# Last stage of a float32 model kernel: matmuls on quarter and eighth tiles without zero halves, one sine operation, and one addition moved from POOL to PE

## The reference

```python
DIM = 128; DEPTH = 6; HEADS = 16; DIM_HEAD = 64; WINDOW = 32; QK_SCALE = 8.0
for i in range(DEPTH):
    x = attn_layer(shift_tokens(x), Wqkv[i], q_scale[i], k_scale[i], Wo[i]) + x
    x = ffn_layer(shift_tokens(x), ln_g[i], ln_b[i], W1[i], b1[i], W2[i], b2[i]) + x
# attn_layer, for q (and k with 1 / scale):
q = l2norm(q) * q_scale
q = q * cos * scale + rotate_half(q) * sin * scale
# local_attention: each window of 32 queries sees its own and the previous window's keys (64)
sim = einsum('bhwie,bhwje->bhwij', bq, bk2) * QK_SCALE      # masked
out = einsum('bhwij,bhwje->bhwie', softmax(sim), bv2)
```

## Time and profile before

| | us |
|---|---|
| median of 3 runs | 4824.44 |
| lowest, highest | 4803.81, 4836.79 |
| profiled execution, span from first to last instruction | 4799.2 |
| PE busy | 4554.0 (95%) |
| DVE busy | 3761.7 (78%) |
| POOL busy | 3692.6 (77%) |
| ACT busy | 3501.1 (73%) |

### The profile page before, as it was taken

How to read it: one execution, slowest core, us unless ns; L and a number is a source line. 1 busy time by engine, 2 the same in 40 slices (tenths; PEclk the granted TensorE clock), 3 DMA queues, 4 the chain that set the end, 5 groups by cost and what they waited for, 6 DMA issues and landing times.

```text
span 4799.2 us, 114895 instructions
## 1 busy us (share of the span) xinstructions
PE 4554.0 (95%) x44512; PEld 3128.6 (65%) x44512; DVE 3761.7 (78%) x5226; ACT 3501.1 (73%) x6738; POOL 3692.6 (77%) x2336
## 2 busy tenths in 40 slices
PE   7998999987887799999999999999999999999997
PEld 5666768874443466666666666666666666666665
DVE  6776556658999688888888888888888888888885
ACT  3454756557775688888888888888888888888885
POOL 2222334438998999999999999999999999999993
PEclk9898999998999999999999999999999999999998
DMA  2000000004332222232222322232322322322222
GB/s 79 1 2 1 2 1 1 1 1 168 150 142 106 55 63 63 56 85 70 54 67 65 75 68 55 68 75 61 68 64 67 76 53 66 80 64 63 62 56 52
DMA packets 164292, 289.06 MB, mean 60 GB/s; under 512 B 44063, under 2 KB 61351, under 8 KB 159655
## 3 DMA queue, kind: packets, MB, share of 16 engines
q1 hardware_dynamic: 162310, 281.46, 22.3%
q10 hardware_dynamic: 1440, 0.24, 0.0%
HBM read 90.22 MB, written 2.62 MB: 19 GB/s over the span
## 4 chain that ended last, share of the span: by engine, by line
PE 59%; ACT 3%; issue 2%; DVE 1%; POOL 1%; ACTq 0%; DVEq 0%; POOLq 0%
PE ps L2559 18%; PE ps L2614 8%; PE ps L2588 8%; PE ps L2572 7%; PE ps L2627 7%; PE ps L2601 3%; PE ps L2669 3%; PE ps L2660 3%; PE ps L2653 3%; ACT L3f_pT L2820 2%; PE ps L2634 1%; PE ps L2640 1%; ACT L3f_kT L2803 1%; POOL L3f_t L3155 0%; POOL L3f_raw L3172 0%
## 5 line engine op out<-in xcount | busy, mean ns | idle before, releaser
L3155 POOL TENSOR_TENSOR L3f_t<-L3f_raw,L3f_rot 128x512 f32<-128x512 f32 x768 | 1007.7, 1334 | 268.3 <-DVE L3f_raw L2971 268.3
L2559 PE MATMUL ps<-L3f_wqkv,all_z 128*128 128x512 f32 x2304 | 1133.7, 601 | 12.8 <-DVE L3f_raw L2971 11.7
L3172 POOL TENSOR_TENSOR L3f_raw<-L3f_raw,L3f_t 128x1024 f32<-128x1024 f32 x384 | 961.4, 2504 | 3.8
L3164 POOL TENSOR_TENSOR L3f_raw<-L3f_raw,L3f_rot 128x1024 f32<-128x1024 f32 x384 | 953.8, 2484 | 3.8
L2971 DVE TENSOR_TENSOR L3f_raw<-ps,L3f_ri 128x512 f32<-128x512 f32 x768 | 495.6, 682 | 231.9 <-ACT L3f_ri L2778 230.2
L2954 DVE TENSOR_REDUCE L3f_ss<-L3f_sqr 128x8 f32<-128x512 f32 x768 | 507.8, 681 | 163.2 <-ACT L3f_sqr L2768 160.8
L2572 PEld LDWEIGHTS ps<-all_ident,L3f_raw 128*128 128x128 f32 x3072 | 358.7, 141 | 320.7 <-issue 282.8
L2559 PEld LDWEIGHTS ps<-L3f_wqkv,all_z 128*128 128x128 f32 x2304 | 385.2, 191 | 221.0 <-issue 151.5
L2572 PE MATMUL ps<-all_ident,L3f_raw 128*128 128x128 f32 x3072 | 472.3, 276 | 49.1 <-ACT L3f_kT L2803 27.1
L2820 ACT ACTIVATE L3f_pT<-ps 64x512 f32<-64x512 f32 x768 | 453.2, 590 | 83.9 <-PE ps L2601 75.9
L2768 ACT ACTIVATE L3f_sqr<-ps 128x512 f32<-128x512 f32 x768 | 449.9, 599 | 76.5 <-PE ps L2559 71.7
(11 more groups left out here) (333 smaller groups left out, 8702.0 us busy)
## 6 DMA issues: line engine op xcount, KB each, us to landing
L3f_vw<-L3f_v SPq DMA_DIRECT2D x1344, 128.0 KB, 2.4
L3a_Bs<-L3a_rows SPq DMA_DIRECT2D x16, 2048.0 KB, 7.1
L3a_Cs<-L3a_rows SPq DMA_DIRECT2D x16, 2048.0 KB, 11.6
L3f_vw<-L3f_v SPq DMA_DIRECT2D x192, 64.0 KB, 2.1
L3f_wqkv<-in_L_ffn_Wqkv SPq DMA_DIRECT2D x24, 256.0 KB, 2.9
L3f_wqkv<-in_L_ffn_Wqkv SPq DMA_DIRECT2D x6, 512.0 KB, 3.6
L3f_wo<-in_L_ffn_Wo SPq DMA_DIRECT2D x48, 64.0 KB, 2.3
out<-all_x SPq DMA_DIRECT2D x8, 256.0 KB, 3.6
```

The lines of the kernel that those rows point to most:

```text
L2559: p.matmul(PS[:, j % 3, :], Z[:, u % NSEQ, t * P:t * P + P], w, start=True, stop=True).then_inc(proj.sem)
L3155: op = g.tensor_tensor(t[:, :, to], r[:, :, fr], w[:, 1, to].unsqueeze(1).broadcast_to((P, H, WIN)), ALU.mult)
L3164: g.tensor_tensor(r, r, w[:, 0, :].unsqueeze(1).broadcast_to((P, H, HD)), ALU.mult).then_inc(cosined.sem)
L3172: g.tensor_tensor(r, r, t, ALU.add).then_inc(rotated.sem)
```

## The change

- `qz` becomes `qT`, the transposed queries with no zeros, and `pT` likewise. `scores` now issues, for each pair of heads and window, one matmul per head: 64 rows by 32 columns of weights, 64 moving columns, output in 32 partitions, one PSUM bank per head. That is 64 matmuls instead of 32, over 2 x 4 = 8 different parts of the array. `values` issues 64 matmuls instead of 32: 64 rows by 64 columns of weights, 32 moving columns, over 2 x 2 = 4 parts.
- ACT's copy of queries is one operation of 128 partitions instead of two of 64, and `spread` one of 128 x 1024 instead of four of 64 x 512.
- The two operations of `sine` become one, which reads the two 32-wide blocks of each head in reverse order.
- For k1, POOL's `add` is gone. PE transposes the cosine part (in `raw`) and then the sine part (in a third buffer of `t2`) into the same place in PSUM, adding. `sine` of k1 now waits for PE's last transpose of k1 of the unit before.
- Mask, scores and probabilities have another order of heads, and the two memsets of zeros are gone.

```diff
-        t2 = self.sb("t2", [P, 2, INNER])
+        t2 = self.sb("t2", [P, 3, INNER])
-        qz = self.sb("qz", [P, TILES, PAIRS, NW, 2, WIN])
+        qT = self.sb("qT", [P, TILES, PAIRS, P])
-        pT = self.sb("pT", [P, TILES, 2 * PAIRS, 2, 2, WIN])
-        oT = self.sb("oT", [P, TILES, PAIRS // 2, NW, 2, WIN])
+        pT = self.sb("pT", [P, TILES, PAIRS, P])
+        oT = self.sb("oT", [P, TILES, 2, PAIRS // 2, P])
...
                 for c in range(4):
-                    mm = p.transpose(PS[:, 3, c * P:c * P + P], raw[:, t, (4 * g + c) * P:(4 * g + c + 1) * P], ident[:, :])
+                    o = PS[:, 3, c * P:c * P + P]
+                    if t and g >= 2:
+                        n = 4 * (g - 2) + c
+                        p.matmul(o, raw[:, t, (4 * g + c) * P:(4 * g + c + 1) * P], ident[:, :], start=True, stop=False, is_transpose=True)
+                        mm = p.matmul(o, t2[:, 2, n * P:(n + 1) * P], ident[:, :], start=False, stop=True, is_transpose=True)
+                    else:
+                        mm = p.transpose(o, raw[:, t, (4 * g + c) * P:(4 * g + c + 1) * P], ident[:, :])
...
                 for a in range(PAIRS):
                     for w in range(NW):
-                        r = slice(w % 2 * HD, w % 2 * HD + HD)
-                        mm = p.matmul(PS[r, 6 + w // 2, a * KEYS:(a + 1) * KEYS], qz[:, t, a, w, :, :].rearrange("p h q -> p (h q)"),
-                                      kT[:, a, t * P + w * WIN:t * P + w * WIN + KEYS], start=True, stop=True)
+                        for h, (r, _) in enumerate(halves):
+                            mm = p.matmul(PS[w * WIN:(w + 1) * WIN, 6 + h, a * KEYS:(a + 1) * KEYS], qT[r, t, a, w * WIN:(w + 1) * WIN],
+                                          kT[r, a, t * P + w * WIN:t * P + w * WIN + KEYS], start=True, stop=True)
...
                     for w in range(NW):
-                        for r in range(2):
-                            a = 2 * c + r
-                            mm = p.matmul(PS[r * HD:(r + 1) * HD, 4 + c // 2, (c % 2) * 256 + w * HD:(c % 2) * 256 + (w + 1) * HD],
-                                          vw[:, u % 2, t * NW + w, a * HD:(a + 1) * HD],
-                                          pT[:, t, w // 2 * PAIRS + a, w % 2, :, :].rearrange("p h q -> p (h q)"), start=True, stop=True)
+                        for to, n in halves:
+                            a = 2 * c + n
+                            for h, (r, _) in enumerate(halves):
+                                mm = p.matmul(PS[to, 4 + h, c * P + w * WIN:c * P + (w + 1) * WIN], vw[r, u % 2, t * NW + w, a * HD:(a + 1) * HD],
+                                              pT[r, t, a, w * WIN:(w + 1) * WIN], start=True, stop=True)
...
-                    for half in range(2):
-                        r = slice(half * HD, half * HD + HD)
-                        op = a.activation(qz[r, t, 4 * g:4 * g + 4, :, half, :], src[r, :, :].rearrange("p c (w q) -> p c w q", q=WIN), ACT.Copy)
+                    op = a.activation(qT[:, t, 4 * g:4 * g + 4, :], src, ACT.Copy)
...
-                for r in range(2):
-                    for half in range(2):
-                        op = a.activation(pT[half * HD:(half + 1) * HD, t, r:2 * PAIRS:2, :, half, :],
-                                          PS[r * HD:(r + 1) * HD, 4:6, :].rearrange("p b (n w h q) -> p (b n) w h q", w=2, h=2, q=WIN)[:, :, :, half, :], ACT.Copy)
-                op.then_inc(pT_in.sem)
+                a.activation(pT[:, t, :, :].rearrange("p a q -> p (a q)"), PS[:, 4:6, :].rearrange("p b n -> p (b n)"), ACT.Copy).then_inc(pT_in.sem)
...
-                for half in range(2):
-                    to, fr = slice(half * WIN, (half + 1) * WIN), slice((1 - half) * WIN, (2 - half) * WIN)
-                    op = g.tensor_tensor(t[:, :, to], r[:, :, fr], w[:, 1, to].unsqueeze(1).broadcast_to((P, H, WIN)), ALU.mult)
-                op.then_inc(sined.sem)
+                else:
+                        g.wait_ge(*qk_turned.at(u - 1, 7))
+                g.tensor_tensor(t.rearrange("p h (b e) -> p h b e", b=2), r.rearrange("p h (b e) -> p h b e", b=2)[:, :, ::-1, :],
+                                w[:, 1, :].rearrange("p (b e) -> p b e", b=2).unsqueeze(1).broadcast_to((P, H, 2, HD // 2)), ALU.mult).then_inc(sined.sem)
...
-                g.tensor_tensor(r, r, w[:, 0, :].unsqueeze(1).broadcast_to((P, H, HD)), ALU.mult).then_inc(cosined.sem)
+                g.tensor_tensor(r, r, w[:, 0, :].unsqueeze(1).broadcast_to((P, H, HD)), ALU.mult).then_inc((rotated if x == "k1" else cosined).sem)
...
-            add(2 * i + 2, "k1")
...
-            add(2 * i + 3, "k1")
```

More of the change, by code:

```diff
@@ L2600, in turn_p @@
                 for n in range(PAIRS):
-                    mm = p.transpose(PS[:, 4 + n // 4, (n % 4) * P:(n % 4 + 1) * P], sm[:, t, 2 * n:2 * n + 2, :].rearrange("p a k -> p (a k)"), ident[:, :])
+                    mm = p.transpose(PS[:, 4 + n // 4, (n % 4) * P:(n % 4 + 1) * P], sm[:, t, n, :, :].rearrange("p h k -> p (h k)"), ident[:, :])
                 mm.then_inc(p_turned.sem)
@@ L2626, in project_out @@
                     for h in range(2):
-                        mm = p.matmul(PS[:, 4, 0:SEQ], wo[:, c, h, :], oT[:, :, c, :, h, :], start=(c + h == 0), stop=(c + h == PAIRS // 2))
+                        mm = p.matmul(PS[:, 4, 0:SEQ], wo[:, c, h, :], oT[:, :, h, c, :], start=(c + h == 0), stop=(c + h == PAIRS // 2))
                 mm.then_inc(w_mm.sem)
@@ L2809, in exponent @@
                 a.wait_ge(*s_sub.at(u, t))
-                a.activation(sm[:, t, :, :], sm[:, t, :, :], ACT.Exp, scale=QK_SCALE).then_inc(s_exp.sem)
+                x = sm[:, t, :, :, :].rearrange("p a h k -> p (a h k)")
+                a.activation(x, x, ACT.Exp, scale=QK_SCALE).then_inc(s_exp.sem)
             def spread(u, t):
@@ L2829, in output @@
                     a.wait_ge(*w_mm.at(u - 1))
-                a.activation(oT[:, t, :, :, :, :].rearrange("p c w h q -> p (c w h q)"), PS[:, 4:6, :].rearrange("p b n -> p (b n)"), ACT.Copy).then_inc(oT_in.sem)
+                a.activation(oT[:, t, :, :, :].rearrange("p h c q -> p (h c q)"), PS[:, 4:6, :].rearrange("p b n -> p (b n)"), ACT.Copy).then_inc(oT_in.sem)
             def centred(u):
@@ L3013, in scale @@
                 v.wait_ge(*s_inv.at(u, t))
-                v.tensor_tensor(sm[:, t, :, :], sm[:, t, :, :], sl[:, t, :].unsqueeze(2).broadcast_to((P, H, KEYS)), ALU.mult).then_inc(s_mul.sem)
+                x = sm[:, t, :, :, :].rearrange("p a h k -> p (a h) k")
+                v.tensor_tensor(x, x, sl[:, t, :].unsqueeze(2).broadcast_to((P, H, KEYS)), ALU.mult).then_inc(s_mul.sem)
             def residual(u):
@@ L3138, in half_of @@
                 c = "qk".index(x[0])
-                return heads(raw[:, int(x[1]), c * INNER:(c + 1) * INNER]), heads(t2[:, c, :]), rot[:, u // NSEQ % 2, int(x[1]), 2 * c:2 * c + 2, :]
+                return heads(raw[:, int(x[1]), c * INNER:(c + 1) * INNER]), heads(t2[:, 2 if x == "k1" else c, :]), rot[:, u // NSEQ % 2, int(x[1]), 2 * c:2 * c + 2, :]
             def sine(u, x):
@@ L3148, in sine @@
                 g.wait_ge(*normed.at(u, 2 * i + 1))
-                if i >= 2:
-                    g.wait_ge(*rotated.at(u, i - 2))
+                if x == "q1":
+                    g.wait_ge(*rotated.at(u, 0))
                 elif u:
-                    g.wait_ge(*rotated.at(u - 1, i + 2))
-                for half in range(2):
-                    to, fr = slice(half * WIN, (half + 1) * WIN), slice((1 - half) * WIN, (2 - half) * WIN)
-                    op = g.tensor_tensor(t[:, :, to], r[:, :, fr], w[:, 1, to].unsqueeze(1).broadcast_to((P, H, WIN)), ALU.mult)
-                op.then_inc(sined.sem)
+                    if x == "q0":
+                        g.wait_ge(*rotated.at(u - 1, 2))
+                    elif x == "k0":
+                        g.wait_ge(*rotated.at(u - 1, 1))
+                    else:
+                        g.wait_ge(*qk_turned.at(u - 1, 7))
+                g.tensor_tensor(t.rearrange("p h (b e) -> p h b e", b=2), r.rearrange("p h (b e) -> p h b e", b=2)[:, :, ::-1, :],
+                                w[:, 1, :].rearrange("p (b e) -> p b e", b=2).unsqueeze(1).broadcast_to((P, H, 2, HD // 2)), ALU.mult).then_inc(sined.sem)
             def cosine(u, x):
@@ L3197, in pool @@
             add(2 * i + 4, "k0")
-        g, v = nc.gpsimd, nc.vector
-        g.memset(vw[:, :, 0, :], 0.0).then_inc(zeroed.sem)
-        g.memset(kT[:, :, 0:WIN], 0.0)
-        g.memset(qz[:, :, :, :, :, :], 0.0)
-        v.memset(pT[:, :, :, :, :, :], 0.0)
+        nc.gpsimd.memset(vw[:, :, 0, :], 0.0).then_inc(zeroed.sem)
+        nc.gpsimd.memset(kT[:, :, 0:WIN], 0.0)
         for k in range(-1, N + 4):
@@ L3230, in constants @@
     first = seen & ((p[:, None] >= 32) | (k >= 32))
-    local = np.where(np.stack([first, seen], 1), 0.0, NEG).astype(np.float32)
-    local = local.reshape(2, 2, 1, 32, TILES, 64).repeat(2, axis=2)
```

(2 more changed lines are left out.)

18 lines of the change are left out of this document (9 added, 9 removed).

## The result

The changed kernel takes **4944.24 us** (median of 4 runs, 4941.51 to 4960.81) against 4818.90 us (4803.81 to 4836.79) for the kernel before. The ratio is 1.0275, with a 95% interval of 1.0238 to 1.0311. I forecast 4642 us and put slower at 0.12: the forecast was wrong, in sign too.

The account below looks back on a forecast made before the run. PE was taken to bound the 66.0 us round of the last stage; PE's sum gave 60.8, but DVE's chain 62.2, so 3.8 us x 48 = 182 us less: 4824 - 182 = 4642 us, range 4535 to 4770.

Parts of the forecast that it names:

- slower at 0.12: Whole kernel: the chance given to a slower result, that of rivals 5 and 6 together.
- Instruction loads: PE's instruction queue: records grow by a factor of 1.57, but the queue's share is 0.5%, so the cost is nothing.
- the price of `values`: PE, values: 128 passes of 32 columns over four parts take 1.23 us a group, 0.79 less.
- scores, 4 groups: PE, scores: 128 passes of 64 columns over eight parts take 1.08 us a group, 0.94 less.
- transposes of k1: PE, k1's second transposes: 16 per round at 0.109 us each, 1.74 us more.
- sum for PE: PE's terms in a round of the last stage: -5.2 us, so 66.0 becomes 60.8 us.
- DVE's chain: DVE's work plus two waits for ACT sets the round at 62.2 us; the forecast itself, 4642 us, chance 0.48.
- rival 3: PE: half of the gain, as values gains nothing or scores runs four parts at a time; 64.0 us, 4728, chance 0.12.
- my lower bound (1.28): PE, scores and values: passes start 10 ns or less apart, one after another, 1.28 us for 128.
- rival 6: PE: each pass has its own price, 0.032 us, so each group takes 4.0 us; some 5680 us, chance 0.06.
- Rival 5: PE: no more side by side than now, groups stay at 2.02 us, transposes add 84; 4908 us, chance 0.06.
- Rival 6's second figure, 5430: PE: with the skill's 25 ns between starts, a group takes some 3.3 us and the kernel about 5430.

Follow-up runs that it names:

- x7: The kernel before, with k1's eight blocks of a unit transposed twice by PE while POOL still adds: +58 us (43 to 74).
- x10: The changed kernel with 129 satisfied waits once ahead of the first group of scores, which became 65 records and shifted PE's list; no time is given.
- x3: The changed kernel with the old values (zero halves, 64 passes of 64 columns): 121 us less than the changed kernel.
- x5: The kernel before with only scores in eight parts and the one sine; old values, POOL's additions kept: 40 us faster than the kernel before.
- x6: The changed kernel with values' weights of 32 columns instead of 64, computing half the output features: 46 us less than the changed kernel.
- x4: The changed kernel with one group of scores and its transposes of the probabilities moved away from values in PE's list: 4992 us.
- x8: x5 with each group of scores cut in halves, a projection or a block of transposes between: 4849 us, 80 us more.
- x9: The kernel before with two satisfied waits ahead of each matmul of scores and values: groups take 3.4 to 3.7 us instead of 1.86; no total is given.

## Why the prediction was wrong

Two steps failed. The one that turned a gain into a loss is **"Instruction loads ... the queue has a share of 0.5%, so this is nothing"**: a term put at nothing, which measured 3.8 us a round in stops. The other is the price of `values`, 0.79 us less a group, which measured nothing. The terms of a round, as forecast and as measured:

```
term                       forecast   measured, us a round
scores, 4 groups              -3.76   -2.36  (1.86 to 1.27, the shortest groups)
values, 4 groups              -3.16    0.0   (1.86 to 1.85)
transposes of k1              +1.74   +1.2   (x7)
stops for instructions         0      +3.8
sum for PE                    -5.2    +2.6
low clock behind the stops     0      up to +0.8  (estimate)
the round                     -3.8    +3.2   (65.9 to 69.2)
```

The last-but-one term is an estimate: (85 - 10) us of the stage at half the clock lose half of that at most, so 37 us in 48 rounds. The sum of the terms is then 3.4 at most, against 3.2 in the profiled executions and 125 / 48 = 2.6 by the medians of the runs, so it closes to some half a microsecond and no better. On average a group of `scores` takes 1.34 us without its stops of over 0.12 us, which would make its term -2.0. The forecast of -3.8 for the round was DVE's chain, not PE's sum.

- **Instruction supply.** A share of queue time is no measure here. What counts is instructions per us where they are densest: a group of 256 in 1.3 to 1.85 us, against a packet of 256 every 3.2 us at best. Before, a group had 128 instructions and the fetches never came below 3.7 us. Shown by x10 and by the place of the stops; what it costs, by x3, x5 and x6. It turned a gain of 1.2 us a round (-2.36 and +1.2) into a loss of 2.6 or more. The Trainium skill, "Runtime: NRT & Kernel Launch", under Instruction fetch mechanics, says that the fetch of instructions is hidden because the sequencer dispatches more slowly, some 20 cycles an instruction. The trace disagrees: 256 instructions in 1.27 us are 5 ns each, and the fetches are not hidden.
- **`values`.** I priced a pass by its moving columns alone. One pass in each part costs 58 ns together with 64 or 32 moving columns, and 34 ns with weights half as wide (x6): the 64 columns of weights are the longer side, and the change left them as they were. Taking the zeros off the moving side could save nothing. My rival 3 had this result for `values`, by a floor of the narrow pass. The rule that I gave for it, Instruction Overhead of "TensorEngine Tiling (Array Packing)" in the Trainium skill, has a pass of 32 moving columns cost as much as one of 60. The gain did stay away, as by that rule, but the trace does not bear out its reason: with 32 moving columns in both, four passes take 58 ns or 34 ns, by the weights.
- **`scores`.** Eight parts do run side by side, the first passes of a group start some 7 ns apart. Then the gaps are longer, and a pass starts every 10 ns on average, so 1.27 us a group at best, the figure of my lower bound (1.28), not 1.08. What sets the 10 ns no run separates. It is not the 25 ns between starts that the Trainium skill gives, "TensorE: Matmul & The Clock Gate", under "Wait — 56ns, not 53.3ns?" (rival 6). The direction was right, and with the one sine worth 40 us (x5).
- **Transposes.** The price of 0.109 each holds, but 0.5 us a round of PE's idle time took part of it (x7).
- **ACT, POOL, DVE.** ACT 334.54 us of 528, in 7.75 rounds by the count of matmuls (9622 of 1242 a round), is 43.2 a round, forecast 44.0; POOL 53.6, as forecast; DVE 52.7. All near, POOL's by luck in part: its sines took 2.59 us and not 2.48, its additions 2.36 and not 2.50, and the two cancel. None mattered, since PE stayed the bound. DVE's chain of 62.2 us was never reached and stays untested.
- **The rivals.** Rival 5 (slower, 4908) was nearest in time, by a mechanism that was not the one, so the closeness is luck: `scores` did get shorter, and `values` stayed at 2.0 by its weights and not for want of overlap. None of the six had the supply of instructions. Rival 6's second figure, 5430, comes out at some 5410 by its own terms.

Still open: whether a list with the same work could avoid the stops without new waits. x4 and x8 tried one way each, and both lost.

## What to carry to other kernels

Before splitting passes over parts of PE's array, count instructions per us where PE's list is densest, loads and neighbours included, and compare with the least distance of the instruction queue's packets. Ask of each small pass whether its weights or its moving columns are longer, and cut only the longer. "Issue" in the middle of a group without waits, ending a fixed time after an instruction packet and always at the same place of 256 records, is the sign of a starved sequencer.

## What the runs showed of the hardware

- PE was supplied with one packet of 256 instructions per 3.2 us at best (3.23 to 3.34 in the eight kernels with such stops); in the changed kernel a stop ended 2.2 to 3.0 us after the start of a fetch.
- Every stop of over 0.5 us inside a group, 680 in eight kernels, stands 193 records behind a multiple of 256 in PE's list.
- The first passes into eight different parts start 7 ns apart; 128 of them 10 ns apart on average at best (1.27 us), weight loads included.
- With 32 moving columns, passes with weights of 64 rows by 64 columns in four parts take 58 ns for the four, by 32 columns 34 ns (x6).
- Two satisfied waits ahead of each small matmul (two passes) stand as one record and cost PE about 50 ns, although nothing is waited for (x9).
- The granted clock fell from 1.00 to 0.50 behind long stops of PE: 85 us of the last stage in the changed kernel, 133 in x6, 10 in the kernel before and in x3, x8 and x9. Six projection passes took 4.27 us there instead of 2.58. So a stop can cost more than its own length.
